# A fused Mamba, LoRA and expert block: two of three state sums as accumulating DMAs from GpSimd, the softplus sum on VectorE, a second fold on GpSimd

## The reference, cut to what matters

```python
delta = softplus(dt @ Wdt.T + dt_bias)
def step(state, xs):
    d_t, B_t, C_t, u_t = xs
    dA = exp(d_t[..., None] * A)
    state = dA * state + (d_t * u_t)[..., None] * B_t[:, None, :]
    y_t = einsum('bdn,bn->bd', state, C_t)
    return state, y_t
y = ys + u * D_param
y = y * silu(gate)
return y @ W_out.T
```

## Time and profile before

| | us |
|---|---|
| median of 3 runs | 2444.64 (2443.39 to 2446.38) |
| the profiled execution | 2442.7 |
| its span | 2440.9 |
| mean granted clock of PE | 0.962 |

### The profile page before, as it was taken

How to read it: one execution, slowest core, us unless ns; L and a number is a source line. 1 busy time by engine, 2 the same in 40 slices (tenths; PEclk the granted TensorE clock), 3 DMA queues, 4 the chain that set the end, 5 groups by cost and what they waited for, 6 DMA issues and landing times.

```text
span 2440.9 us, 30553 instructions
## 1 busy us (share of the span) xinstructions
PE 2240.2 (92%) x10140; PEld 1900.0 (78%) x10140; DVE 2229.0 (91%) x2104; ACT 1614.2 (66%) x3763; POOL 2116.4 (87%) x1090
## 2 busy tenths in 40 slices
PE   8989999999899998999989999999989977787879
PEld 7777878888678877888868887788878765666767
DVE  1389999999999999999999999999999999998892
ACT  1467667776777667776677667776677666765550
POOL 0189889999999999999899999999899999999870
PEclk9999999999999999999989998999999998989989
DMA  7454445444454444544455433644345332632342
GB/s 227 143 202 109 139 137 172 150 138 132 125 191 154 147 139 158 165 147 139 136 168 161 148 130 118 208 159 136 117 165 161 122 108 70 202 104 96 112 139 97
DMA packets 133178, 352.15 MB, mean 144 GB/s; under 512 B 38733, under 2 KB 43341, under 8 KB 131549
## 3 DMA queue, kind: packets, MB, share of 16 engines
q1 hardware_dynamic: 110254, 298.28, 37.9%
q10 hardware_dynamic: 22768, 51.93, 6.2%
HBM read 339.14 MB, written 11.02 MB: 143 GB/s over the span
## 4 chain that ended last, share of the span: by engine, by line
PE 42%; POOL 22%; DVE 21%; issue 9%; ACT 6%; DMA 1%; ACTq 0%; SPq 0%; DVEq 0%; POOLq 0%
POOL st L1530 12%; DVE scan L1303 11%; PE late L692 8%; PE ubank L638 7%; PE ubank L611 7%; POOL st L1538 6%; PE gbank L590 3%; DVE st L1315 3%; DVE ubank L1284 2%; PE scan L611 2%; DVE scan L1313 2%; ACT L1223 2%; POOL st L1544 2%; ACT scan L1133 2%; PE gbank L655 2%
## 5 line engine op out<-in xcount | busy, mean ns | idle before, releaser
L1530 POOL TENSOR_TENSOR st<-w_sb,bc 128x1024 f32<-128x1024 f32 x512 | 1198.0, 2357 | 122.7 <-PE gbank L655 110.3
L1303 DVE TENSOR_TENSOR_SCAN scan<-scan,st 128x1024 f32<-128x1024 f32 x512 | 1167.5, 2288 | 33.9 <-ACT scan L1133 18.4
L1133 ACT ACTIVATE scan<-delta,A_sb 128x255 f32<-128x255 f32 x2048 | 846.1, 459 | 0.1
L1538 POOL TENSOR_TENSOR st<-st 128x1024 f32<-128x1024 f32 x255 | 601.1, 2357 | 20.8 <-DVE st L1315 10.8
L611 PE MATMUL ubank<-h,wt 128*128 128x256 f32 x1712 | 423.3, 404 | 93.1 <-ACT qg L1223 87.6
L638 PE MATMUL ubank<-h,wt 128*128 128x256 f32 x2048 | 471.2, 384 | 23.2 <-ACT qg L1223 23.2
L611 PEld LDWEIGHTS ubank<-h,wt 128*128 128x128 f32 x1712 | 345.2, 204 | 161.8 <-ACT qg L1223 109.2
L638 PEld LDWEIGHTS ubank<-h,wt 128*128 128x128 f32 x2048 | 393.6, 193 | 81.7 <-ACT qg L1223 27.2
L1315 DVE TENSOR_TENSOR st<-scan,bc 128x1024 f32<-128x1024 f32 x384 | 453.8, 1208 | 0.0
L692 PE MATMUL late<-yg,wt 128*128 128x256 f32 x1792 | 407.1, 386 | 26.3 <-DVE x L1340 22.1
L1130 ACT ACTIVATE scan<-iota 128x4 f32<-128x4 f32 x512 | 86.9, 170 | 491.7 <-DVE st L1315 455.9
(11 more groups left out here) (219 smaller groups left out, 2257.1 us busy)
## 6 DMA issues: line engine op xcount, KB each, us to landing
wt<-in_W_in SPq DMA_DIRECT2D x256, 512.0 KB, 3.6
wt<-in_W_out SPq DMA_DIRECT2D x132, 512.0 KB, 3.4
wt<-in_cond_W SPq DMA_DIRECT2D x64, 512.0 KB, 3.6
bc<-bc_rows ACTq DMA_DIRECT2D x64, 512.0 KB, 6.8
wt<-G_tiles SPq DMA_DIRECT2D x32, 512.0 KB, 3.6
wt<-in_ffn_B SPq DMA_DIRECT2D x20, 512.0 KB, 3.6
xb<-in_x SPq DMA_DIRECT2D x8, 1024.0 KB, 7.1
x<-in_x ACTq DMA_DIRECT2D x28, 256.0 KB, 4.0
```

The lines of the kernel that those rows point to most:

```text
L1133: last = fn(t[:, k, 1:T], delta[:, c, 1:T], ACT.Exp, scale=A_sb[:, col:col + 1])
L1303: v_.tensor_tensor_scan(Tps[q % 2][:, :], Tps[q % 2][:, :], x_, 0.0, ALU.mult, ALU.add).then_inc(scan_done, 1)
L1530: tt(st[:, n % ST_RING, :, :], w_sb[:, i % 2:i % 2 + 1, :].to_broadcast([P, NQ, T]), bc[:, 0, q * NQ:(q + 1) * NQ, :], ALU.mult).then_inc( ...
L1538: tt(st[:, n % ST_RING, :, :], st[:, n % ST_RING, :, :], st[:, (n - 1) % ST_RING, :, :], ALU.add).then_inc(add_done, 1)
```

## The change

1. `add_first` on DVE and the second `add` on POOL are gone. In their places POOL issues a DMA (`add_dma`, L1552) that adds one plane of `st` onto the next in SBUF (`accum_op=ALU.add`, 128 x 1024): quarter 0 onto 1, and quarter 2 onto 3. `add` on POOL (quarter 1 onto 2) stays. Each kind has a semaphore of its own (`acc_st`).
2. POOL folds twice, to one plane of 256 columns, and PE sums with one identity matmul.
3. The sum in softplus moves from POOL to DVE: ACT writes abs(z) to `delta` and log(1 + exp(-abs)) over it; DVE's `delta_sum` (L1310) computes max(z, 0) + delta with z from PSUM. ACT's relu is gone, and so are `tmp` and POOL's `delta_add`.
4. `ST_RING` is 8, and the wait for `id_mm` stands before quarter 3. `fold` of chunk i-1 stands in iteration i, after two `dbu`. On DVE `mul(i, 0)` stands before `scan(i, 1)`.
5. The conditioning jobs are spread: tiles 0 and 1 (and the adapter "la") go to chunks 13 to 15 of the batch before, from chunks 3 and 5 (and 14); tiles 2 and 3 are made in two halves in chunks 5 and 6, and 7 and 8 (`small_begun`, `cond_begin`).
6. Loads of B rows, of x and stores of the output are issued at other points, singly; `wT` shares the memory of `la`; the experts' weights are spread with a column of the identity (two matmuls of 64 columns) where a selection matrix did it (one of 128).

```diff
 def half_job(i):
-    if f and c <= 2:
-        return ("Bs", f - 1, 5 + c)
...
-    if j < B and c in (3, 5, 7, 8, 9, 11):
-        return ("cond", j, {3: 0, 5: 1, 7: 2, 8: 3, 9: 5, 11: 7}[c])
...
+    if f and c <= 3:
+        return ("Bs", f - 1, 4 + c)
...
+    if j < B and c in (9, 11):
+        return ("cond", j, {9: 5, 11: 7}[c])
+    if c >= 13 and b + 3 < B:
+        return (("la", b + 3, 0), ("cond", b + 3, 0), ("cond", b + 3, 1))[c - 13]
...
             def sum_states(i):
-                pe.wait_ge(add_done, 3 * i + 3)
+                pe.wait_ge(add_done, 2 * i + 2)
...
-                for k in range(2):
-                    last = mm(gbank[:, 0:T], ident[:, :], st[:, n % ST_RING, k, :], start=(k == 0), stop=(k == 1))
-                last.then_inc(id_mm, 1)
+                mm(gbank[:, 0:T], ident[:, :], st[:, n % ST_RING, 0, :], start=True, stop=True).then_inc(id_mm, 1)
...
+            def delta_sum(b, j):
+                job = ("dt", b, j)
+                n = 8 * b + j
+                d = delta[:, 2 * j:2 * j + 2, :].rearrange("p c t -> p (c t)")
+                dve.wait_ge(sp_step, 3 * n + 3)
+                v_.scalar_tensor_tensor(d, home(job)[:, :], 0.0, d, ALU.max, ALU.add).then_inc(delta_done, 1)
+                dve.wait_ge(delta_done, n + 1)
+                dve.sem_inc(ev_inc(job), 1)
...
-            def add(i, k):
+            def add_dma(i, k):
+
                 n = 4 * i + k
+                pool.wait_ge(mul_done, n + 1)
                 if k == 3:
-                    pool.wait_ge(add_done, 3 * i + 1)
+                    pool.wait_ge(add_done, 2 * i + 1)
+                pool.dma_start(st[:, n % ST_RING, :, :], st[:, (n - 1) % ST_RING, :, :], accum_op=ALU.add
+                               ).then_inc(acc_st[k // 2], 16)
+
+            def add(i):
+                n = 4 * i + 2
+                pool.wait_ge(acc_st[0], 16 * (i + 1))
                 pool.wait_ge(mul_done, n + 1)
                 tt(st[:, n % ST_RING, :, :], st[:, n % ST_RING, :, :], st[:, (n - 1) % ST_RING, :, :], ALU.add
                    ).then_inc(add_done, 1)
 
             def fold(i):
                 t = st[:, (4 * i + 3) % ST_RING, :, :]
-                pool.wait_ge(add_done, 3 * i + 2)
-                tt(t[:, 0:2, :], t[:, 0:2, :], t[:, 2:4, :], ALU.add).then_inc(add_done, 1)
-
...
+                pool.wait_ge(acc_st[1], 16 * (i + 1))
+                tt(t[:, 0:2, :], t[:, 0:2, :], t[:, 2:4, :], ALU.add).then_inc(fold_done, 1)
+                pool.wait_ge(fold_done, i + 1)
+                tt(t[:, 0, :], t[:, 0, :], t[:, 1, :], ALU.add).then_inc(add_done, 1)
```

174 lines of the change are left out of this document (84 added, 90 removed).

## The result

| | before | after |
|---|---|---|
| median, us | 2445.3 (2443.4 to 2446.4, 4 runs) | 2538.8 (2535.8 to 2541.1, 4 runs) |
| the profiled execution's span, us | 2440.9 | 2538.4 |
| mean granted clock of PE | 0.962 | 0.937 |

A forecast was written before the change was run, and what follows sets the result against it. DVE was taken to bound the kernel, POOL close behind; after the change POOL's 271 us a batch would. Savings of 54 us in batches 1 to 6, 9 in batch 0 and 3 in batch 7 gave 2378 us, range 2335 to 2540.

The forecast's parts named there:

- floor of 269.4 us a batch: DVE in a middle batch: 281.2 less 20.2 for `add_first`, plus 6.4 for `delta_sum` and 2 for waits on scans.
- DVE sets the pace: Rival: an issue takes 0.8 us or less on POOL, DVE's 267 us a batch remain, 2346 us; chance 0.20.
- An issue: POOL issuing one accumulating DMA: taken as 1.1 us, two a chunk, between POOL's operations of 256 and 512 columns.
- theory C: Theory held in the experiments, on POOL: an issue of an accumulating DMA costs it more than 1.1 us.
- The cycle: POOL's work in a chunk: 14.55 us without the DMAs plus 2.2 for two issues, 16.75 us, or 268.0 a batch.
- The landing: Accumulating DMA from issue to landed: taken as 5.3 us, hidden on average, with 0.2 us a chunk of waits on POOL.
- the landing is late: Rival: landings take 7.1 us, POOL waits 1.4 and 0.6 us, its chunk is 18.75 us, 2586 us; chance 0.20.
- L = 6.5: Time from issue to landed at which POOL's chunk is again 17.57 us and the change turns to a loss.
- the maximum of two engines: Summing step: a middle batch takes the larger of POOL's 271 us and DVE's 269.4, so 271.
- The DMA share: DMA engines' busy share in a middle batch: up from 47% to 66% to 84% with the accumulations' 16.8 MB.
- The fit: The skill's rule for GpSimd DMAs: 2.0 us plus bytes over 436 GB/s, 3.2 us for 512 KB, 4.4 for 1024 KB.
- The lock rival: DVE's two-port mode keeps POOL from writing descriptors, each issue waits half a scan, 2635 us; chance 0.02.

The follow-up runs named there:

- e15: The changed kernel without the two accumulating DMAs and the waits for their landings (two of four sums missing from the result): 2343.6 us.
- e17: The changed kernel with each accumulating DMA replaced, at its place, by POOL's own add of half the columns, the other half left out: 2412.7 us.
- e4: The changed kernel with POOL's second fold alone undone, so that PE sums two planes with two identity matmuls: 2474.4 us.
- e7: The changed kernel with PE's half job of a chunk moved ahead of its wait for the fold at `sum_states`: 2551.2 us.
- e12: The changed kernel with POOL's own `add` of each chunk made half as wide, so the output is not the reference's: 2444.5 us.

## Why the prediction was wrong

**DVE: right.** Its floor of 269.4 us a batch stood at 266.9 to 270.5 in batches 1 to 6 of e15. That e15's 2343.6 us lie so near the 2346 of the rival "DVE sets the pace" is partly luck: that rival had 267 us a batch, 1602 for batches 1 to 6, and e15 took 1615.8; from batch 7 on it had 338, and e15 took 314.7. `delta_sum` took 0.67 us, as said.

**An issue: right in its sum, not in its make-up.** (16.85 - 14.55) / 2 gives 1.15 us each against my 1.1, and theory C falls. But the sign that the prediction named, start to start of the instruction behind the DMA, reads 0.61 us (1468.12 to 1468.73). The rest is in the instructions behind an issue (two products of 4.94 us against 4.68, `weight` below) and in the 0.63 us that stand ahead of each second issue. The 0.8 and 1.2 us around my value are durations of other operations, so that 1.1 came out is partly luck. The 0.33 us that it gives for the other queues' issues is the shortest of the earlier trace rows; the medians there are 0.35 and 0.66.

**The cycle: right.** 16.85 us against 16.75. The windows that cover a landing are 5.6 and 6.3 us, against 5.7 and 6.5.

**The landing: the step that failed.** "It is hidden on average, with 0.2 us a chunk for landings behind bursts of loads (rows of B take 6.8 us), 3 us a batch." The median was right (5.3), and the median is not what POOL pays. A landing that comes before its window's end gives nothing back; POOL pays one that comes late whole. 43 of 128 first landings and 33 of 127 second ones were late, by 2.0 us on average ((94.9 + 55.9) / 76) and 5.2 at most. In batches 1 to 6 POOL's list of waits reads:

```profile
POOL st L1559 <- DMA st<-st: 84.4, 35, 5.2
POOL st L1552 <- POOL st L1559: 54.6, 81, 0.9
POOL st L1565 <- DMA st<-st: 42.5, 26, 4.7
POOL st L1543 <- PE gbank L664: 31.1, 12, 6.2
POOL st L1552 <- DVE st L1331: 10.1, 15, 0.8
```

The first and the third row are 127 us, or 21 a batch, where the prediction had 3. The rival "the landing is late" named the right mechanism and the right place, and was priced by shifting the median to 7.1. Its turning point, L = 6.5 or 0.8 us of waits a chunk, was sound: 1.2 was measured. The text also said what would prove it wrong, "if POOL's waits name the DMA st<-st for more than 1 us a chunk", and that is what they do. The measured 2538.8 us lie 1 us inside the range's upper end, 2540, which had been set for the milder half of the late landings: the range had taken the rival in, the forecast had the direction wrong.

**The second step that failed: the maximum of two engines.** The sum took the larger of POOL's 271 and DVE's 269.4. Under "What bounds the kernel now" it says of POOL's waits for PE that they "cost little as POOL works ahead". That was true of a POOL with slack. Once POOL sets the pace, its waits for others are in the time too: 41 us in batches 1 to 6 (31.1 + 10.1). Even without a landing (e17) a middle batch takes 280, not 273.

**The account for batches 1 to 6.** Predicted 1626 us, measured 2202.2 - 416.1 = 1786.1, taken from the first scans of batches 1 and 7. POOL's work 96 x 16.85 = 1617.6, its landings 126.9, PE and DVE 41.2: 1785.7. Against the prediction: 10 for the cycle, 109 for landings, 41 for the other waits. Batch 0 took 297.0 (predicted 285), batch 7 with the tail 336.3 (predicted 344); these nearly cancel.

**PE: right in its size, wrong in its worth.** "Its total was not the limit" holds: e4 gave it more work and was faster. But its in-order stop at `sum_states`, 221.5 us in 64 waits, stands in no step of the prediction. The change puts `fold` of chunk i-1 behind two `dbu` of the next iteration, and little is left between its end and `y_sum`: in the rows of after POOL's delay reaches DVE in the same chunk. I hold this for the reason why POOL's and DVE's waits do not hide each other, but no run shows it. e7 shows only that PE's order isn't the cause; a version with the fold early again wasn't run. PE's clock is a second open point: in a batch of e15 1203 records kept PE busy for 260.0 us at a granted clock of 0.98, in batch 3 of after 1202 records for 269.6 us at 0.93. In e12, which leaves PE's work as it is and waits less for POOL, batch 3 ran at 0.96 (1201 records, 266.0 us). So the clock goes with the waiting here, and what the slower matmuls add to the kernel's time in turn isn't separated by any run; in POOL's account it can stand in the 41 us of waits for PE and DVE alone.

**The DMA share: right.** 0.68 to 0.72 in batches 1 to 6 against 0.66 to 0.84. Weights' landings went from 3.6 to 4.5 us at the median, and PE's longest total wait for weights was 15.0 us in 4 waits: as expected, PE did not suffer.

**The fit, and the lock.** By the fit of the Trainium skill (DMA: Bandwidth & Descriptors, Anatomy of one DMA — SWDGE (gpsimd) path) the sum would have been 3 us a batch lower. The shortest of the trace's 255 landings took 4.37 us, about its 4.4 for 1024 KB, but the fit says nothing on what a landing beside other loads takes, and that was what counted. The lock rival did not come true: POOL's 255 issues take 856 to 983 ns, all of them, beside busy scans.
